# A Mamba block with a routed mixture of experts on one core: VectorE's small routing and root operations alternated with convolution taps and each other

## The reference, cut to what matters

```
# layer 1, d_inner = 512
xs, z = split(x @ W_in.T)
xc  = silu(causal_conv(xs, 4 taps) + conv_b)
a   = softplus((xc @ W_x.T)[:, :32] @ W_dt.T + b_dt)
x   = layernorm(x + x + (xc * a * silu(z)) @ W_out.T)
# layer 2, 16 experts in 4 groups
scores = sigmoid(x @ gate_w.T);  sfc = scores + gate_bias
group score = sum of the two best sfc of a group; keep the best 2 groups
chosen = the 4 best sfc in the kept groups; cw = 2.5 * scores / sum(chosen scores)
y  = sum over chosen e of cw[e] * (silu(x @ Wg[e]) * (x @ Wu[e])) @ Wd[e]
y += (silu(x @ Ws_g) * (x @ Ws_u)) @ Ws_d
x  = layernorm(x + x + y)
```

## Time and profile before

| | |
|---|---|
| median of 3 runs | 575.7 us (575.3 to 576.9) |
| profiled execution, span | 575.4 us |
| TensorE busy | 526.5 us (91%) |
| VectorE busy | 435.1 us (76%) |
| ScalarE busy | 373.4 us (65%) |
| GpSimd busy | 333.5 us (58%) |
| first stage up to the last transposes | 300.46 us |
| mean granted clock of TensorE | 0.981 of full speed |

### The profile page before, as it was taken

How to read it: one execution, slowest core, us unless ns; L and a number is a source line. 1 busy time by engine, 2 the same in 40 slices (tenths; PEclk the granted TensorE clock), 3 DMA queues, 4 the chain that set the end, 5 groups by cost and what they waited for, 6 DMA issues and landing times.

```text
span 575.4 us, 11796 instructions
## 1 busy us (share of the span) xinstructions
PE 526.5 (91%) x3133; PEld 445.1 (77%) x3133; DVE 435.1 (76%) x1114; ACT 373.4 (65%) x962; POOL 333.5 (58%) x368
## 2 busy tenths in 40 slices
PE   5898899899999999999859898999999999889793
PEld 5686676677867778676648788999999998889682
DVE  4896799999999999999895477444444458888586
ACT  4694848668486683855623575677867777667453
POOL 3503102376675766856576667777777766666730
PEclk9999899999999999999989999999999999999898
DMA  7993303243241423313696647976666688884895
GB/s 178 311 288 120 113 38 123 73 144 121 72 169 65 155 90 111 118 53 109 199 384 222 220 157 248 328 246 207 208 203 197 196 319 275 297 294 174 323 383 201
DMA packets 70726, 111.21 MB, mean 193 GB/s; under 512 B 12708, under 2 KB 54053, under 8 KB 70152
## 3 DMA queue, kind: packets, MB, share of 16 engines
q1 hardware_dynamic: 53880, 71.37, 38.9%
q0 software_dynamic: 13056, 35.68, 16.7%
q10 hardware_dynamic: 3728, 3.42, 1.7%
HBM read 61.77 MB, written 50.74 MB: 196 GB/s over the span
## 4 chain that ended last, share of the span: by engine, by line
PE 47%; DVE 31%; issue 12%; ACT 3%; POOL 3%; DMA 2%; ACTq 0%; DVEq 0%; POOLq 0%
DVE xc L1398 6%; PE psum L957 6%; PE psum L958 5%; PE psum L959 5%; PE psum L939 5%; PE psum L743 4%; PE psum L981 3%; PE psum L983 3%; PE psum L982 3%; DVE sp L1420 3%; PE psum L967 3%; POOL x_buf L632 2%; PE psum L1060 2%; DVE m L1424 2%; PE psum L682 2%
## 5 line engine op out<-in xcount | busy, mean ns | idle before, releaser
L632 POOL DMA_INDIRECT x_buf<-row,row_id x128 | 131.5, 1027 | 63.4 <-issue 36.0
L674 POOL DMA_INDIRECT y_buf<-y_out,y_ids x96 | 96.6, 1006 | 46.1 <-issue 26.2
L624 POOL TENSOR_TENSOR m<-xc,zs 128x512 f32<-128x512 f32 x32 | 41.5, 1315 | 89.2 <-DVE shift L1460 43.2
L1779 DVE TENSOR_TENSOR t_lo<-psum,t_hi 128x512 fp32r<-128x512 f32 x72 | 48.7, 684 | 54.9 <-ACT t_hi L1247 54.9
L957 PE MATMUL psum<-ew_gu_hi,t_hi 128*128 x288 | 85.0, 295 | 2.1 <-DVE t_lo L1779 1.0
L958 PE MATMUL psum<-ew_gu_lo,t_hi 128*128 x288 | 81.5, 283 | 0.0
L959 PE MATMUL psum<-ew_gu_hi,t_lo 128*128 x288 | 81.4, 283 | 0.0
L1398 DVE SCALAR_TENSOR_TENSOR xc<-psum,cw_taps,xc 128x511 f32<-128x511 f32 (+2 forms) x96 | 71.6, 747 | 7.7 <-ACT halo_x L1084 5.4
L957 PEld LDWEIGHTS psum<-ew_gu_hi,t_hi 128*128 128x128 f32 x288 | 55.0, 191 | 5.7 <-issue 4.3
L682 PE MATMUL psum<-x_hi,win_hi 128*128 128x512 f32 x128 | 53.8, 420 | 1.5 <-issue 1.5
L958 PEld LDWEIGHTS psum<-ew_gu_lo,t_hi 128*128 128x128 f32 x288 | 55.1, 191 | 0.0
(11 more groups left out here) (244 smaller groups left out, 1352.6 us busy)
## 6 DMA issues: line engine op xcount, KB each, us to landing
tiles_in<-x_buf SPq DMA_DIRECT2D x144, 144.0 KB
y_in<-y_buf SPq DMA_DIRECT2D x32, 512.0 KB, 8.6
xT<-in_x_T SPq DMA_DIRECT2D x8, 512.0 KB, 3.9
xtok<-in_x_tok SPq DMA_DIRECT2D x8, 512.0 KB, 3.4
gu_hi_buf<-w_hi_now SPq DMA_DIRECT2D x8, 512.0 KB, 3.1
out_dram<-res ACTq DMA_DIRECT2D x6, 512.0 KB, 6.8
x_buf<-pad_row SPq DMA_DIRECT2D x17, 144.0 KB
raw_gu<-in_wg_T SPq DMA_DIRECT2D x16, 128.0 KB, 3.4
```

Source lines behind the costliest of these rows:

```text
L632: nc.gpsimd.indirect_dma_start(out=x_buf, out_offset=bass.IndirectOffsetOnAxis(ap=row_id[t % ROWS][:, b, k:k + 1], axis=0), in_=row[t % RO ...
L674: nc.gpsimd.indirect_dma_start(out=y_buf, out_offset=bass.IndirectOffsetOnAxis(ap=y_ids[:, q % IDS, i:i + 1], axis=0), in_=y_sent[:, i, :] ...
```

## The change

The small operations become functions of one operation each, with a wait in front of the operation that needs it (`seen`) in place of one behind the operation that gives it. `tile(t)` on VectorE is rewritten with them: route and pick of tile t-1 alternate with convolution taps and norm statistics, choose up to `sel` alternates with the inverse root. The second half of choose (weights and slots into the rows) becomes seven functions, called one tile later beside the residual of t-2, which moves ahead of the softplus. The semaphore of place is its own (`place_step`). The turn's list (t = 7) is rewritten in the same manner: rows and place of tile 5 alternate with the halves of its residual, and route, pick and choose of tile 6 with the norm of tile 7; and `fill_rows(7)` (those seven again) follows `choose(7)` in the second stage. TensorE's tiles 1 to 6 take `out_proj_by_pairs`. ScalarE takes `gate_exp` before the second `log_part`. GpSimd's wait for `y_done` goes.

```diff
@@ GpSimd, tile
-                    at_least(pool, "y_done", PAIRS * t + 1)
                     gate_product(t, range(2, KI))
@@ TensorE
             def out_proj_by_pairs(t):
+                if t < NT - 1:
+                    at_least(pe, "sp_done", PAIRS * (t + 1))
                 for i in range(PAIRS):
@@ TensorE, tile
-                out_proj(t)
+                out_proj_by_pairs(t)
@@ ScalarE, tile
                 abs_part(t, range(2, KI))
+                gate_exp(t - 1)
                 log_part(t, range(2, KI))
-                gate_exp(t - 1)
@@ VectorE
+            def mark(ins, name):
+                counted[name] += 1
+                ins.then_inc(s[name], 1)
+            def seen(name, but=0):
+                dve.wait_ge(s[name], counted[name] - but)
...
+            def group_ties(t):
+                seen("route_step")
+                mark(V.tensor_tensor(cmp_b, cmp_b, before[:, :, :].unsqueeze(1).to_broadcast([P, SUB, NG, NG]),
+                                     ALU.mult), "route_step")
...
+            def tile(t, more=True):
+                n, r, p = t + 1, t - 1, t - 2
+                placed = p >= 0
+                if placed:
+                    weigh_chosen(p)
+                    slot_chosen(p)
+                    residual_half(p, 0)
+                    weight_sum(p)
+                    slots_to_rows(p)
+                    weight_guard(p)
+                    residual_half(p, 1)
+                    weight_norm(p)
+                softplus_sum(t, 0)
+                if placed:
+                    weights_to_rows(p)
+                softplus_product(t, 0)
+                gate_logits(r)
+                conv(n, 0)
+                softplus_sum(t, 1)
+                gate_one(r)
+                softplus_product(t, 1)
+                gate_score(r)
+                conv_tap(n, 1, 1)
+                if placed:
+                    place_rank(p)
+                gate_biased(r)
+                conv_tap(n, 1, 2)
+                if placed:
+                    place_rows(p)
+                group_pairs(r)
+                conv_tap(n, 1, 3)
+                if placed:
+                    place_top(p)
+                group_sums(r)
+                conv_halo(n, 0)
+                if placed:
+                    place_ids(p)
+                group_score(r)
...
+                shared_act(r, 0)
+                conv_tap(n, 2, 1)
+                group_compare(r)
+                conv_tap(n, 2, 2)
+                group_ties(r)
+                conv_tap(n, 2, 3)
+                group_better(r)
+                norm_sum(t, 0)
+                group_rank(r)
+                norm_stats(t, 0)
+                group_cap(r)
...
+                norm_sum(t, 1)
+                pick_kept(r)
+                norm_stats(t, 1)
+                pick_top(r)
+                for b in range(SUB):
+                    norm_mean(t, b)
+                choose_compare(r)
+                norm_var(t)
+                choose_place(r)
+                root_bits(var[:, :], half_bits[:, :], "norm_step")
+                choose_above(r)
+                root_guess(rstd[:, :], half_bits[:, :], "norm_step")
+                choose_order(r)
+                root_z(var[:, :], **root)
+                choose_ties(r)
+                root_h(**root_of)
+                choose_sel(r)
+                root_once(**root_of)
+                root_h(**root_of)
+                root_series(root_z_[:, :], root_h_[:, :], "norm_step")
+                root_series_end(root_z_[:, :], root_h_[:, :], "norm_step")
+                root_last(**root)
+                norm_shift(t)
+                conv(n, 3)
+                conv_halo(n, 1)
+                shared_act(r, 1)
+                x1T_low(t)
+                dt_low(n)
+                if more:
+                    x_low(t + 2)
@@ VectorE, the turn (t = 7, r = t - 1)
+            softplus(t, 0)
+            gate_logits(r)
+            softplus_sum(t, 1)
             for i in PIECES_OF[TABLE_TILE - 1]:
                 weights_low(i)
+            gate_one(r)
+            softplus_product(t, 1)
+            gate_score(r)
+            shared_act(r, 0)
...
+            choose_compare(r)
+            root_guess(rstd[:, :], half_bits[:, :], "norm_step")
+            choose_place(r)
+            root_z(var[:, :], **root)
...
+            root_last(**root)
+            weight_sum(r)
+            norm_shift(t)
```

More of the change, by code:

```diff
@@ L1517, in pick, with gate_one, gate_score, gate_biased @@
-            def pick(t):
+            def gate_one(t):
+                dve.wait_ge(s["gate_exp"], t + 1)
+                mark(V.tensor_scalar(flat(sfc[:, :, :]), flat(score[:, :, :]), 1.0, None, ALU.add), "route_step")
+            def gate_score(t):
+                seen("route_step")
+                mark(V.reciprocal(flat(score[:, :, :]), flat(sfc[:, :, :])), "route_step")
+            def gate_biased(t):
+                seen("route_step")
+                mark(V.tensor_tensor(sfc[:, :, :], score[:, :, :],
+                                     gbias[:, :].unsqueeze(1).to_broadcast([P, SUB, E]), ALU.add), "route_step")
@@ new lines, in pick_top, with pick, choose_compare @@
+                    mark(V.max(top8[:, b, :], picked[:, b, :]), "route_step")
+            def pick(t):
+                group_compare(t)
+                group_ties(t)
+                group_better(t)
+                group_rank(t)
+                group_cap(t)
+                pick_kept(t)
+                pick_top(t)
+            def choose_compare(t):
+                fourth = top8[:, :, TOP - 1:TOP].to_broadcast([P, SUB, E])
+                seen("route_step")
+                mark(V.tensor_tensor(equal[:, :, :], picked[:, :, :], fourth, ALU.is_equal), "route_step")
+                mark(V.tensor_tensor(above[:, :, :], picked[:, :, :], fourth, ALU.is_gt), "route_step")
@@ new lines, in choose_ties, with choose_sel @@
+            def choose_ties(t):
+                seen("route_step")
+                mark(V.scalar_tensor_tensor(posn[:, :, :], posn[:, :, :], float(TOP), equal[:, :, :],
+                                            ALU.is_le, ALU.mult), "route_step")
+            def choose_sel(t):
+                seen("route_step")
+                V.tensor_tensor(sel[:, :, :], posn[:, :, :], above[:, :, :], ALU.add).then_inc(s["sel_done"], 1)
+            def choose(t):
+                choose_compare(t)
+                choose_place(t)
+                choose_above(t)
+                choose_order(t)
+                choose_ties(t)
+                choose_sel(t)
@@ L1578, in place, with place_rows, place_top, place_ids @@
                      .then_inc(s["cut_done"], 1)
[L1579 to L1580 removed]
+            def place_rows(t):
+                seen("place_step", 1)
+                mark(V.scalar_tensor_tensor(posn[:, :, :], posn[:, :, :], 1.0, sel[:, :, :],
+                                            ALU.add, ALU.mult), "place_step")
+            def place_top(t):
+                seen("place_step")
                 for b in range(SUB):
[L1583 removed]
+                    mark(V.max(pos8[:, b, :], posn[:, b, :]), "place_step")
+            def place_ids(t):
+                seen("place_step")
                 V.tensor_scalar(row_id[t % ROWS][:, :, :], pos8[:, :, 0:TOP], 1.0, None, ALU.subtract).then_inc(s["routed"], 1)
[L1585 removed]
+            def place(t):
+                place_rank(t)
+                place_rows(t)
+                place_top(t)
+                place_ids(t)
             table_n = [0]
@@ L1817, in norm @@
                 first, end = NORMS[k]
-                n, steps = end - first, NORM_STEPS * k
+                n = end - first
                 aggregate(k, range(first + aggregated, end))
                 at_least(dve, "o_agg", end)
-                V.tensor_scalar(o_var[:, 0:n], o_mv[:, 0:n, 1], EPS, None, ALU.add).then_inc(s["o_norm"], 1)
-                dve.wait_ge(s["o_norm"], steps + 1)
+                mark(V.tensor_scalar(o_var[:, 0:n], o_mv[:, 0:n, 1], EPS, None, ALU.add), "o_norm")
                 if k >= 2:
@@ L1894, in _ @@
                 turned_low(0, 0, k)
-            choose(t - 1)
+            weight_guard(r)
+            slots_to_rows(r)
+            weight_norm(r)
+            weights_to_rows(r)
             x1T_low(t)
-            place(t - 1)
-            residual(t - 1)
+            place(r)
+            residual(r)
             each_quad(iteration)
```

372 lines of the change are left out of this document (224 added, 148 removed).

## The result

The changed kernel takes 578.98 us (578.87 to 579.21, four runs) against 576.24 (575.3 to 576.9, four runs). The ratio on record is 1.0052, interval 1.0032 to 1.0071; that of these two medians is 1.0048. In a second series it was 1.004, 1.0025 to 1.0055. It is slower by about half of one per cent, and 578.3 was forecast. The sum came out; one of its terms has the wrong sign, and others made up for it.

What follows compares the result with a forecast made beforehand. The path from second softplus sum through `shift` to normalization closes the tile, TensorE arriving together. Tile 1 +0.7, tile 2 -1.1, tiles 3 to 5 +3.6, tile 6 +1.5, turn -2.2: +2.5 on 575.7, say 578.3; range 573.8 to 582.3.

Steps and rivals of the forecast that it cites:

- The bound: Steady tile: softplus sum, `shift`, normalization close it at 35.10 us, with TensorE's route arriving together; TensorE alone needs 34.4.
- What a wait costs: VectorE's small operations: each broken wait gives 0.12 us, some 37 in a steady tile, 4.4 us.
- The start of the sum: Second softplus sum on VectorE: starts at T + 16.95, T being the start of the previous tile's transposes, 0.23 earlier.
- The segment: Second softplus sum to `shift`: 16.9 us, not 15.45; +1.2 a tile, +3.6 for tiles 3 to 5, +1.5 for tile 6.
- list of signs: Expected in the trace: tiles 3 to 5 36.2 to 36.4 apart, idle 1.5 to 2.2, turn 30.5 to 31.
- rival on the faster side: Six tiles: VectorE's segment is shorter than summed; from 0.4 shorter no slower, at 1.5 shorter 570.6 us; chance 0.15.
- Tiles 1 and 2: First two tiles, up to their transposes: tile 1 +0.7 us, tile 2 -1.1 us.
- The turn: Last tile of the first stage: VectorE's serial 12.62 us to `shift` becomes 10.5 by alternation; -2.2, between -1.5 and -3.
- hidden by the same slack: GpSimd's gate product, without its wait, starts up to 1 us earlier beside VectorE's product, at no cost.
- The clock: TensorE's new idle, some 1.9 us in four tiles and 3 in tile 6; a clock fall would cost 1.6 each.
- the rival: TensorE's clock falls in tile 6 and sometimes before: +1.6 to +4.8 us, 580 to 583; chance 0.17.
- The pairs and the residual's wait: TensorE's product and residual waits, taken as 0.3 and 0.4 us a tile, go; both gains vanish into the normalization wait.

Runs made afterwards that it cites:

- behind_wait: `behind` with GpSimd's wait for VectorE's first product put back: 572.28 us, 0.9924 of the kernel before.
- best: `pool_wait` with small operations reordered into waiting gaps or before the second softplus sum, weight piece and table steps behind `shift`: 566.33 us, 0.9819 of the kernel before.
- behind: The changed kernel with route, pick and choose up to `sel` of tiles 1 to 6 put back behind `shift`: 587.48 us, 1.0167 of the kernel before.
- each_waits: `pool_wait` in its own order, with every small operation of route, place, norm and root waited for at once: 629.11 us, 1.0897 of the kernel before.
- pool_wait: The changed kernel with one line put back, GpSimd's gate product waiting again for VectorE's first product: 574.14 us, 0.9975 of the kernel before.
- before_no_wait: The kernel before with only GpSimd's wait for `y_done` taken out of its tile: 595.31 us, 1.0313 of the kernel before.

## Why the prediction was right, and where not

- **The bound.** Right: the path from the second softplus sum over `shift` to the normalization closes the tile. The idle before the transposes, foretold at 1.5 to 2.2 and 3 in tile 6, is 1.34 to 1.38 and 2.38; `behind_wait` takes the moved operations off and it is gone. TensorE's own period was put at 34.4 and is 34.31 in `best`. But the path is not the only bound: without the alternation VectorE's whole round is one as well, as `behind` shows, full at 36.8.
- **What a wait costs.** Right: 0.12 was foretold, and `each_waits` has 0.09 to 0.14 for each of some 38. The rule of the Trainium skill that was weighed (VectorE: DVE Perf Modes, The DRAIN you can't avoid: semaphores cost nothing) does not hold for these operations on 4 to 64 elements. The section measured it on eight `tensor_copy`, and it says too that a next operation that is not held starts earlier, which is what the rows 0.07 and 0.14 apart show; the prediction weighed its first half only.
- **The start of the sum**, T + 16.95: measured 16.79, VectorE 1.01 idle (1.05 foretold). Right.
- **The segment**, 16.9: measured 16.43. Too large by 0.5, and 0.15 more was allowed for a stretched instruction. With the start's 0.16 this makes 35.54 and not 36.3 a tile: +1.5 for tiles 3 to 5 instead of +3.6, and +0.6 instead of +1.5 for tile 6. A mis-sized term; the sign and the place were right. By the prediction's own list of signs the tiles miss (36.2 to 36.4 apart, idle 1.5 to 2.2), and so does the turn (30.5 to 31, measured 33.6). Its rival on the faster side says that from 0.4 a tile shorter than the sum the kernel is no slower. The tiles were 4.0 shorter in all, so that rival had come true, and the kernel is slower because the turn was lost: `pool_wait`, with the same tiles, is at 0.9975.
- **Tiles 1 and 2**: +0.5 (+0.7 foretold) and -1.9 (-1.1): a difference of periods; the end of tile 2 came 1.4 earlier than before, 0.4 was foretold.
- **The turn**, -2.2: measured +0.7. This is the step that failed. Its chain was even shorter than foretold (9.74 for 10.5), and with the wait back the turn is 29.9, -3.0. What failed is the sentence that GpSimd's product "loses its wait for `y_done` and starts up to 1 us earlier beside VectorE's product: hidden by the same slack". It starts 4.2 us earlier in the turn (278.75 for 282.92), 4.9 counted from T, and it is not harmless there: it holds a VectorE operation for 2.5, and TensorE's clock takes 1.4 more. I counted an engine's slack and did not ask what else the two engines share. The section on the chip says that the engines wait for each other on semaphores only; the holds show that this is not so. The rows were there, timeline of GpSimd of the kernel before, a steady tile and the turn, with 0.93 and 4.91 us of waiting:

```profile
210.22 2.55 POOL L624 TENSOR_TENSOR m<-xc,zs 128x512 f32<-128x512 f32 x2 [0.93 <-DVE m L1424]
...
282.92 2.50 POOL L624 TENSOR_TENSOR m<-xc,zs 128x512 f32<-128x512 f32 x2 [4.91 <-DVE m L1424]
```

- **The clock.** The new idle of the tiles did not lower it (1.00 in every stretch from 90 to 276 us), as the forecast had it; the rival put the fall in tile 6. It fell in the turn instead, after the idle of 3.60 that the hold made, and once more before the last transposes, as it does in the kernel before. With `before_no_wait` there is one more row: after an idle of 2.21 it fell too, and after 2.38 (tile 6 of the changed kernel) it did not.
- **The pairs and the residual's wait** went into the idle, as foretold.

So +2.5 was forecast and +2.7 came by the medians, +1.8 by the two spans. By the spans the tiles up to the transposes of tile 6 cost 4.0 less than foretold (+0.7 for +4.7) and the turn with what follows 3.3 more (+1.1 for -2.2): two errors of opposite sign. The time was right in part by luck; the mechanism in the tiles was not luck.

The Trainium skill (SBUF — State Buffer, Who interferes with whom) says that VectorE and GpSimd share a pair of ports by an exclusive lock: a VectorE instruction with two inputs from SBUF, or one like `tensor_scalar` in a mode that uses both ports, and a GpSimd instruction that reads SBUF block each other, and whoever comes first keeps it. Every hold here agrees in the operands: tensor_scalar (2.67), its form with two inputs (2.66), `weights_to_rows` (2.56), the product (3.31); and the taps, which read one input from PSUM, take their usual 2.31 for three beside GpSimd's product from 173.76 in the changed kernel. That the tensor_scalar uses both ports is read from its hold alone, as no trace names the mode. Who came first is not shown by the records: the guard starts 0.13 ahead of GpSimd's product and `row<-picked,tok_row` in `before_no_wait` 0.59 ahead, and both are held. How long a hold lasts is open as well. The five long ones last over both of GpSimd's back to back instructions, 2.5 and not 1.3. But `pair_max` of `before_no_wait` is held over the first product only (91.78 to 93.03), and `pair_sum` gets the second (to 94.26). What makes the difference was not found.

## What to carry to other kernels

Before a wait between two engines is dropped as redundant, look at what the engine will run beside, and not at who needs its result: an order that nobody needs for data can keep two engines apart, here for 4.8 us in one kernel and 18 in the other. Small dependent operations on VectorE are cheapest one in each waiting gap of another chain; put more there than there are gaps, or put them on the path that closes the tile while they could stand beside it, and the saving is spent (the change), laid out by gaps, with the wait kept and the weight piece and the table off the path as well, it is 1.8% (`best`, on one chip). And when an order is tried, vary the collision partner too: `behind` alone would have told against a layout that wins by 0.8%.

## What the runs showed of the hardware

- A VectorE operation is held by two GpSimd products that run beside it, whatever its size: 128x4, 128x64 and 128x1024 all lost about the time that was left of them (2.5, 2.35, 2.1), and one of 128x64 in `before_no_wait` 2.95.
- In an alternation a VectorE operation follows one of 64 elements after 0.13 to 0.15 with nothing to wait for and 0.25 to 0.26 with a wait, and one of 4 elements after 0.07 to 0.08 and 0.19 to 0.20 (`pool_wait`, `each_waits`).
- A hold of 2.1 to 2.5 can cost more than itself, as TensorE's clock may fall behind it: 0.9 more in a steady tile of `before_no_wait`, 1.4 in the turn of the changed kernel.
- On one chip the same kernel took 696 us and not 577, with gaps of 0.3 to 1.0 between instructions of VectorE and about 4 on ScalarE. What they wait for was not found.
